# Differential attention on one core: every eighth maximum tile goes through ScalarE and GpSimd

## The reference, cut to what matters

```
q, k = rope(x @ Wq) * 8 ** -0.5, rope(x @ Wk)          # (b, 32, s, 8) each
scores = einsum('bhqd,bhkd->bhqk', q, k)                # 16 x 32 tables of 1024 x 1024
probs = softmax(scores, axis=-1)                        # fp32, over the keys
w = probs[:, :, 0] - lam * probs[:, :, 1]               # the two heads of a pair
attn = einsum('bhqk,bhkd->bhqd', w, v)                  # v has 16 columns
attn = attn * rsqrt(mean(attn ** 2) + eps) * subln_g * (1 - LAMBDA_INIT)
```

## Time and profile before

| | us |
|---|---|
| median of 3 runs (6433.96 to 6452.12) | 6438.76 |
| the profiled execution | 6450.77 |
| its span | 6449.0 |

### The profile page before, as it was taken

How to read it: one execution, slowest core, us unless ns; L and a number is a source line. 1 busy time by engine, 2 the same in 40 slices (tenths; PEclk the granted TensorE clock), 3 DMA queues, 4 the chain that set the end, 5 groups by cost and what they waited for, 6 DMA issues and landing times. The chain is left out here.

```text
span 6449.0 us, 136849 instructions
## 1 busy us (share of the span) xinstructions
PE 5794.4 (90%) x36560; PEld 1816.8 (28%) x36560; DVE 5879.4 (91%) x6456; ACT 4718.1 (73%) x8950; POOL 1947.2 (30%) x3270
## 2 busy tenths in 40 slices
PE   7776999999999999999999999999999999997775
PEld 4442222222222222222222222222222222224423
DVE  7998999999999999999999999999999999986716
ACT  4553878888788888887888888888878888783304
POOL 6774222222222222222222222222222222225506
PEclk8886999999999999999999999999999999998878
DMA  4554222222222222222222222222222222205688
GB/s 145 152 160 121 40 46 48 48 48 50 46 48 48 48 48 48 48 48 48 48 48 48 48 48 48 48 48 48 48 48 48 48 48 48 47 19 179 197 314 282
DMA packets 435720, 491.57 MB, mean 76 GB/s; under 512 B 106451, under 2 KB 288883, under 8 KB 435171
## 3 DMA queue, kind: packets, MB, share of 16 engines
q1 hardware_dynamic: 434147, 483.60, 31.2%
q10 hardware_dynamic: 1024, 0.53, 0.0%
HBM read 360.60 MB, written 123.21 MB: 75 GB/s over the span
## 5 line engine op out<-in xcount | busy, mean ns | idle before, releaser
L650 ACT ACTIVATE at_e<-at_ps_e 128x512 f32<-128x512 f32 x8192 | 4236.1, 602 | 944.1 <-PE at_ps_e L748 943.9
L664 DVE TENSOR_REDUCE at_largest<-at_ps_m 128x1 f32<-128x1024 f32 x4096 | 4777.2, 1211 | 156.4 <-PE at_ps_m L775 95.9
L775 PE MATMUL at_ps_m<-k_stack,q_stack 48*128 48x512 bf16 x8192 | 2725.2, 387 | 159.7 <-DVE at_largest L664 112.3
L748 PE MATMUL at_ps_e<-q_stack,k_stack 51*128 51x512 bf16 x8192 | 2478.6, 383 | 154.3 <-ACT at_e L650 69.1
L763 PE MATMUL at_ps_o<-at_e,at_v 128*32 128x512 f32 x16384 | 2255.2, 623 | 0.1
L748 PEld LDWEIGHTS at_ps_e<-q_stack,k_stack 51*128 51x128 bf16 x8192 | 624.5, 94 | 2520.6 <-ACT at_e L650 2216.6
L580 POOL TENSOR_TENSOR at_negated<-at_zeros,at_largest_t 128x32 f32<-128x32 f32 x256 | 64.8, 253 | 3244.3 <-DVE at_largest_t L671 3244.3
L775 PEld LDWEIGHTS at_ps_m<-k_stack,q_stack 48*128 48x128 bf16 x8192 | 620.1, 93 | 924.0 <-DVE at_largest L664 884.9
L763 PEld LDWEIGHTS at_ps_o<-at_e,at_v 128*32 128x32 f32 x16384 | 450.3, 149 | 525.5 <-issue 340.3
L615 POOL TENSOR_TENSOR at_rms<-at_mean_eps,at_minus_half 128x16 f32<-128x16 f32 x128 | 372.7, 2912 | 10.0
L429 PE MATMUL pr_ps_q<-pr_xn_t,pr_w 128*128 128x512 f32 x512 | 232.8, 597 | 1.5 <-issue 0.8
(11 more groups left out here) (128 smaller groups left out, 3082.2 us busy)
## 6 DMA issues: line engine op xcount, KB each, us to landing
k_stack<-k_parts SPq DMA_DIRECT2D x1536, 64.0 KB
q_stack<-q_parts SPq DMA_DIRECT2D x256, 192.0 KB
q_stack<-q_parts SPq DMA_DIRECT2D x256, 128.0 KB
w_first<-in_w SPq DMA_DIRECT2D x32, 1024.0 KB, 11.7
ex_w_second<-in_w SPq DMA_DIRECT2D x32, 1024.0 KB, 12.7
q_parts<-pr_parts SPq DMA_DIRECT2D x96, 256.0 KB, 2.9
k_parts<-pr_parts SPq DMA_DIRECT2D x96, 256.0 KB, 2.9
pr_x_in<-in_x SPq DMA_DIRECT2D x16, 1024.0 KB, 6.2
```

Source lines behind the costliest of these rows:

```text
L650: nc.scalar.activation(e[:, j % E_BUFS], ps_e[:, (HALVES * u + j) % SLOTS], ACT.Exp, scale=SCALE).then_inc(exp_done, 1)
L664: nc.vector.reduce_max(largest[:, u % 2, j // SIDE, j % SIDE:j % SIDE + 1], ps_m[:, j % 2], AX.X).then_inc(max_done, 1)
L748: nc.tensor.matmul(ps_e[:, (HALVES * u + j) % SLOTS], k_stack[rows, u, pair, c, kt * P:(kt + 1) * P], q_stack[rows, u, pair, c, half * HAL ...
L775: last = nc.tensor.matmul(ps_m[:, j % 2, half * HALF:(half + 1) * HALF], q_stack[rows, u, pair, c, t * P:(t + 1) * P], k_stack[rows, u, pa ...
```

## The change

Tries 0, 8, 16 and 24 of each quad are no longer reduced from PSUM by DVE. ACT copies each (128x1024) from `ps_m` to one of two buffers `fold_in`, after the second exponential of the period in which it is made. POOL folds it: high half minus low half, clamped at zero, added to the low half, which is the larger of the two; once on 512 and once on 256 columns; the result of 256 columns goes to `fold_out`. DVE takes the maxima of two such results in one reduction per side, in `turn_maxima`, and then waits for its own result before the transpose. Side 0 is turned at g = 10 (`TURN`) instead of 8. Maxima are now stored negated (the reductions negate), so `split` has four operations where it had five. POOL's order in a turn is: fold 0, `finish` of the previous quad, fold 1, split of side 0, folds 2 and 3, split of side 1. Try j waits for the copy instead of the reduction where try j-2 is a folded one; the counts in `max_done` are adapted. ACT's loop runs over 31 trips and writes out the last four quads, since the last quad has no tries to copy for.

```
--- before.py
+++ after.py
@@ -44,6 +44,7 @@
 LAMBDA_INIT = 0.8 - 0.6 * math.exp(-0.3 * 12)
 SCALE = HD ** -0.5
 EPS = 1e-5
+LARGEST = float(np.finfo(np.float32).max)
 THETA = 0.0001
 SWAP = [i ^ 1 for i in range(32)]
 
@@ -469,6 +470,18 @@
         BLK = 32
         BLOCKS = HALF // BLK
         loops = quads // BUFS - 1
+        FOLD_EVERY = 8
+        FOLDS = TRIES // FOLD_EVERY
+        WIDTH = S // 4
+        REDUCED = TRIES - FOLDS
+        TURN = TILES + 2
+
+        def folded(j):
+            return j % FOLD_EVERY == 0
+
+        def reduced_before(j):
+            return sum(not folded(i) for i in range(j))
+
         with ExitStack() as ctx:
             def sb(name, shape, dt=F32):
                 return ctx.enter_context(nc.sbuf_tensor("at_" + name, shape, dt))
@@ -480,7 +493,8 @@
             v = sb("v", [P, BUFS, 2, 2 * VD * TILES])
             e = sb("e", [P, E_BUFS, HALF])
             largest, largest_t = sb("largest", [P, 2, 2, BLK]), sb("largest_t", [P, BLK])
-            zeros, negated, rest = sb("zeros", [P, BLK]), sb("negated", [P, BLK]), sb("rest", [P, BLK])
+            zeros, rest = sb("zeros", [P, BLK]), sb("rest", [P, BLK])
+            fold_in, fold_out = sb("fold_in", [P, 2, S]), sb("fold_out", [P, 2, 2, WIDTH])
             parts = sb("parts", [P, PARTS, BLK], BF16)
             sums_t = sb("sums_t", [P, 2, BLOCKS, BLK])
             inverse = sb("inverse", [P, 2, BLOCKS])
@@ -507,8 +521,10 @@
             max_stored, inverse_done, attn_done, out_done = (sem("max_stored"), sem("inverse_done"), sem("attn_done"),
                                                              sem("out_done"))
             out_stored, pool_step = [sem("out_stored0"), sem("out_stored1")], sem("pool_step")
+            copied, fold_done, folds_read = sem("copied"), sem("fold_done"), sem("folds_read")
+            passed = sem("passed")
             ONES = 5
-            SPLIT_STEPS, FINISH_STEPS = 4, 10
+            SPLIT_STEPS, FINISH_STEPS, FOLD_STEPS = 3, 10, 5
             block = ctx.enter_context(nc.Block())
 
             @block.sync
@@ -577,16 +593,35 @@
                 def split(h, base):
 
                     pool.wait_ge(max_turned, h + 1)
-                    nc.gpsimd.tensor_tensor(negated[:], zeros[:], largest_t[:], ALU.subtract).then_inc(pool_step, 1)
                     if not (isinstance(h, int) and h == 0):
                         pool.wait_ge(max_stored, 16 * (P // BLK) * h)
-                    nc.gpsimd.tensor_tensor(parts[:, 0], zeros[:], largest_t[:], ALU.subtract).then_inc(pool_step, 1)
+                    nc.gpsimd.tensor_tensor(parts[:, 0], largest_t[:], zeros[:], ALU.add).then_inc(pool_step, 1)
+                    pool.wait_ge(pool_step, base + 1)
+                    nc.gpsimd.tensor_tensor(rest[:], largest_t[:], parts[:, 0], ALU.subtract).then_inc(pool_step, 1)
                     pool.wait_ge(pool_step, base + 2)
-                    nc.gpsimd.tensor_tensor(rest[:], negated[:], parts[:, 0], ALU.subtract).then_inc(pool_step, 1)
+                    nc.gpsimd.tensor_tensor(parts[:, 1], rest[:], zeros[:], ALU.add).then_inc(pool_step, 1)
                     pool.wait_ge(pool_step, base + 3)
-                    nc.gpsimd.tensor_tensor(parts[:, 1], rest[:], zeros[:], ALU.add).then_inc(pool_step, 1)
-                    pool.wait_ge(pool_step, base + 4)
                     nc.gpsimd.tensor_tensor(parts[:, 2], rest[:], parts[:, 1], ALU.subtract).then_inc(split_done, 1)
+
+                def fold(m, k, base):
+
+                    c, x = k // 2, fold_in[:, k % 2]
+                    pool.wait_ge(copied, FOLDS * m + k + 1)
+                    for width in (S // 2, S // 4):
+                        low, high = x[:, 0:width], x[:, width:2 * width]
+                        nc.gpsimd.tensor_tensor(high, high, low, ALU.subtract).then_inc(pool_step, 1)
+                        pool.wait_ge(pool_step, base + 1)
+                        pool.sem_inc(passed, 1)
+                        nc.gpsimd.tensor_scalar(high, high, LARGEST, 0.0, ALU.min, ALU.max).then_inc(pool_step, 1)
+                        pool.wait_ge(pool_step, base + 2)
+                        if width > WIDTH:
+                            nc.gpsimd.tensor_tensor(low, low, high, ALU.add).then_inc(pool_step, 1)
+                            pool.wait_ge(pool_step, base + 3)
+                            base = base + 3
+                        else:
+                            if not (isinstance(m, int) and m == 0):
+                                pool.wait_ge(folds_read, 2 * m + c - 1)
+                            nc.gpsimd.tensor_tensor(fold_out[:, c, k % 2], low, high, ALU.add).then_inc(fold_done, 1)
 
                 def finish(n, base):
 
@@ -619,36 +654,70 @@
 
                 def turn(n, rows, base):
                     if rows:
-                        for c in range(2):
-                            split(2 * (n + AHEAD) + c, base)
-                            base = base + SPLIT_STEPS
-                    finish(n, base)
-
-                for h in range(2 * AHEAD):
-                    split(h, SPLIT_STEPS * h)
+                        fold(n + AHEAD, 0, base)
+                        base = base + FOLD_STEPS
+                    finish(n - 1, base)
+                    base = base + FINISH_STEPS
+                    if rows:
+                        fold(n + AHEAD, 1, base)
+                        split(2 * (n + AHEAD), base + FOLD_STEPS)
+                        base = base + FOLD_STEPS + SPLIT_STEPS
+                        for k in (2, 3):
+                            fold(n + AHEAD, k, base)
+                            base = base + FOLD_STEPS
+                        split(2 * (n + AHEAD) + 1, base)
+
+                first = FOLDS * FOLD_STEPS + 2 * SPLIT_STEPS
+
+                def first_maxima(m, base):
+                    for c in range(2):
+                        for k in (2 * c, 2 * c + 1):
+                            fold(m, k, base)
+                            base = base + FOLD_STEPS
+                        split(2 * m + c, base)
+                        base = base + SPLIT_STEPS
+
+                first_maxima(0, 0)
+                first_maxima(1, first)
                 pool.wait_ge(lam_done, 1)
-                start, steps = 2 * AHEAD * SPLIT_STEPS, 2 * SPLIT_STEPS + FINISH_STEPS
+                start, steps = 2 * first, first + FINISH_STEPS
                 with hinted(nc, pool, 0, loops) as i:
                     for u in range(BUFS):
-                        turn(BUFS * i + u, True, start + steps * (BUFS * i + u))
+                        turn(BUFS * i + u + 1, True, start + steps * (BUFS * i + u))
                 for u in range(BUFS):
                     n = BUFS * loops + u
-                    turn(n, u < BUFS - AHEAD, start + steps * n - 2 * SPLIT_STEPS * max(0, u - (BUFS - AHEAD)))
+                    turn(n + 1, n + 1 + AHEAD < quads, start + steps * n - first * max(0, n + 1 + AHEAD - quads))
 
             @block.scalar
             def _(act):
+                act.sem_inc(exp_done, SLOTS)
+
+                def copy_trial(m, k):
+
+                    act.wait_ge(tries_done, TRIES * m + FOLD_EVERY * k + 1)
+                    if not (isinstance(m, int) and m == 0 and k < 2):
+                        act.wait_ge(fold_done, FOLDS * m + k - 1)
+                    nc.scalar.copy(fold_in[:, k % 2], ps_m[:, FOLD_EVERY * k % 2]).then_inc(copied, 1)
+
+                def turn(n, u, tries):
+                    for j in range(HALVES):
+                        act.wait_ge(scores_done, HALVES * n + j + 1)
+                        if j % QUAD == 0:
+                            act.wait_ge(sums_done, GROUPS * n + j // QUAD + 1 - E_GROUPS + E_GROUPS)
+                        nc.scalar.activation(e[:, j % E_BUFS], ps_e[:, (HALVES * u + j) % SLOTS], ACT.Exp,
+                                             scale=SCALE).then_inc(exp_done, 1)
+                        if tries and j % QUAD == 1 and folded(2 * (j // QUAD)):
+                            copy_trial(n + AHEAD, 2 * (j // QUAD) // FOLD_EVERY)
+
+                for k in range(FOLDS):
+                    copy_trial(0, k)
                 act.wait_ge(lam_dots, 1)
                 nc.scalar.activation(lam_exp[:], lam_dot[:], ACT.Exp).then_inc(lam_exps, 1)
-                act.sem_inc(exp_done, SLOTS)
-                with hinted(nc, act, 0, loops + 1) as i:
+                with hinted(nc, act, 0, loops) as i:
                     for u in range(BUFS):
-                        n = BUFS * i + u
-                        for j in range(HALVES):
-                            act.wait_ge(scores_done, HALVES * n + j + 1)
-                            if j % QUAD == 0:
-                                act.wait_ge(sums_done, GROUPS * n + j // QUAD + 1 - E_GROUPS + E_GROUPS)
-                            nc.scalar.activation(e[:, j % E_BUFS], ps_e[:, (HALVES * u + j) % SLOTS], ACT.Exp,
```

(24 more changed lines are left out.)

## The result

| | us |
|---|---|
| changed kernel, median of 4 runs (6599.47 to 6617.4) | 6606.98 |
| kernel before, median of 4 runs (6433.96 to 6452.12) | 6439.93 |
| ratio after / before | 1.0258 (1.0236 to 1.028) |
| the profiled execution of the changed kernel, its span | 6611.6, 6609.8 |

Slower by 167 us, 1.3 us for each of the 127 quads with tries. Forecast were 6579 and 1.13 a quad, inside a range of 6440 to 6720. All times and ratios here are of fast executions; one execution of the kernel of experiment 4 took 9511 us and is left out.

What follows compares the result with a forecast made beforehand. A ring through PE and ACT, not DVE, was taken as the bound. -0.90 + 1.78 + 0.25 = +1.13 us a quad, x 127 = +143, -3 at the start: +140 on 6438.8 gives 6579 us; range 6440 to 6720.

Steps and rivals of the forecast that it cites:

- the ring: Attention loop: PE and ACT instructions releasing each other, not through DVE, set 2.42 us a period, 38.77 us a quad.
- Rival 1, the busy shares: Attention loop: DVE at 97% limits and ACT's idle time takes the copies; faster, 6353 us; chance 0.11.
- rival 2: ACT's copies: the copy costs half, about no change, 6445 us; chance 0.05.
- The copy on the ring, 0.45: ACT, four copies a quad: each adds 0.45 us to the ring, 1.78 us a quad.
- DVE's 0.9 us: DVE's extra work (turnings, sums, reciprocal) lengthens some intervals: 0.9 us a quad, all that DVE costs before the change.
- the room at the gate: PE's even try waiting for DVE's reduction: 0.41 us of room, T+0.66 to T+1.07; T starts the period's third score.
- the 0.25: DVE's delays remaining after the change: 0.25 us a quad in place of 0.9.
- DVE's pace: DVE's reductions of tries from PSUM: 1.184 us each, from fourteen in 16.57 us.
- The turning: DVE turning a side's maxima: folded reduction 0.62, wait on its own result 0.1, then transpose; 0.87 us instead of 0.15.
- rival 3: POOL's folds late, DVE waiting: decides at a fold of 6.0 us; 6706 us at 6.5; chance 0.14.
- the end of 5.5: POOL's fold: forecast at 5.1 us, with ends 4.6 and 5.5.
- PE's stops without a releaser: PE's stops, 25 at weight loads, and what follows them: remaining 0.7 us of the 40.4 us quad, left unchanged.

Runs made afterwards that it cites:

- experiment 4: The changed kernel, but ACT copies only 16 of the 1024 columns of each folded try (maxima wrong): 6542 us, 1.0142 of the kernel before.
- experiment 2: Kernel before, tries 0, 8, 16, 24 reduced over 16 columns only and each exponential on 384 of 512 columns: 6328 us, 0.9811.
- experiment 3: Kernel before, with ACT also copying a constant 128x1024 SBUF tile at the change's four places, read by nobody; DVE reduces all 32 tries: 6615 us, 1.0258.
- experiment 1: Kernel before, with tries 0, 8, 16, 24 of each quad reduced over 16 of 1024 columns; no copy, no fold: 6427 us, 0.9967.
- experiment 5: The changed kernel, with side 0 turned in period 12 and POOL folding try 16 before that side's split: 6566 us, 1.0189 of the kernel before.
- experiment 7: The changed kernel, ACT copying only columns 512 to 1023, DVE reducing the rest from PSUM, side 0 turned in period 12: 6432 us, 0.9967 of the kernel before.
- experiment 6: The changed kernel, with one more 128x512 two-input POOL operation in each fold: 6890 us, 1.0686 of the kernel before.
- 8, half copy after extra work: The changed kernel with half copies of tries 0, 4, 16, 20, POOL folding to 64 columns, side 0 turned in period 10: 6362 us, 0.986 of before.

## Why the prediction was right, and where it was not

**The bound.** Right, and shown: the time follows ACT's instruction (experiments 2 and 3), not DVE's work (1). DVE stands close behind: half of what the shorter ring of experiment 2 would give came back as its delays. Rival 1, the busy shares, and rival 2 are out.

**The copy on the ring, 0.45.** Right: 0.46, four times a quad, in the change, and 0.48 with foreign data from SBUF. Of the parts, the pace is 0.89 (3024.35 to 3025.24) and not 0.93, and the group behind the copy makes up for it (2.12 for 2.06). An estimate by the formula of the Trainium skill (ScalarE: Activation LUTs, section What ACT_TABLE_LOAD costs) gives a pace of 0.946. That is above the 0.89 from PSUM and fits the 0.94 of experiment 3 from SBUF; on the ring it would make 0.47 a copy, which these runs can't tell from 0.45.

**DVE's 0.9 us and what is left of it.** The net was right by two errors that met, and that is luck. The step that failed is the room at the gate: I compared the opening of the gate (T+0.66) with the score behind it (T+1.07) and overlooked that the second half of the try must also run before the weighted sums. 0.19 is what there is. With 0.41 I had the relief worth 0.9 us a quad; alone it is worth 0.36 (experiment 1). In the change nearly all of the 0.9 goes all the same, because the copies lengthen the periods in which DVE would be late: alone they leave 0.12 (experiment 3), and with the copies made short the delays are back (experiment 4). So the 0.25 that I put against 0.9 was close to the 0.36 measured, for a reason that the text had only in half: I had seen the shift of T by 0.45 after each copy, and had not seen that this shift does nearly all of it. What the relief adds to it is worth about 0.1 us a quad (0.12 of delays in experiment 3, nothing left in experiment 5), less than the 0.32 that its dearer turning costs.

**DVE's pace.** 1.184 was wrong, 1.12 is right. I divided a stretch of fourteen reductions by fourteen although the first of each pair waits for its data; gaps of a few hundredths don't stand as idle time in a merged row. The sum should have warned me: 40.3 us of DVE's work do not fit into a quad of 39.67.

**The turning.** 0.87 forecast, 1.01 measured: the reduction 0.67 for 0.62, the wait on its own result 0.20 for 0.10. The 0.20 is not the price of that wait alone. In experiment 7 the wait for the side's reductions (`max_done`) stands ahead of the folded reduction instead of behind it, and the transpose starts 0.03 after the reduction's end (3004.77):

```profile
3004.09 0.68 DVE L740 TENSOR_REDUCE at_largest<-at_fold_out 128x2 f32<-128x514 f32 x1
3004.80 0.21 DVE L745 STREAM_TRANSPOSE at_largest_t<-at_largest 128x32 f32<-128x32 f32 x1
```

So the place of that one wait may have cost the change 0.17 us a turning; the two programs differ in more, and no run changes it alone. The dearer turning is the 0.32 at period 10 where 0.2 stood, and experiment 5 takes it away whole. With the 0.06 from four copies and the rest of the delays it makes up the difference of 0.17 us a quad, most of the 28 us between 6579 and 6607.

**POOL.** Covered, as forecast: by 0.34 us and not by 1 until DVE waits, and by 0.8 until it costs time (experiment 6). The 6.0 us at which rival 3 was to decide holds: of the 1.35 us added to a fold, half of 1.91, 0.96, reached the ring, so the loss began at 5.6 + 1.35 - 0.96 = 5.99. The fold's 5.6 is beyond the end of 5.5 that I had given. The two-input operations cost 1.27 and 0.73, not 1.058 and 0.614; the clamp was cheaper than taken (0.61 and 0.40) but starts 0.20 behind the operation before it. The row for 1.058 has one input that is broadcast, and the one for 0.614 reads the same tile twice. The addition of two different halves of a tile, 256 each, was in the profile of before and fitted (724 ns); I took the wrong neighbours:

```profile
L602 POOL TENSOR_TENSOR at_attn<-at_normed 128x256 f32<-128x256 f32 x128 | 92.7, 724 | 10.0
```

The rule of the Trainium skill (GPSIMD Engine Reference, section Engine selection) holds in its part on one input, roughly (0.61 for 512, where DVE's reduction of 512 from SBUF takes 0.67), and by it rival 3 does not occur. It didn't, but a fold is mostly two-input work, and at 5.6 us it was 0.4 short of where the rival begins.

**Small slips in the sums.** With a pace of 0.946 for 0.93 a quad is 0.064 longer, 8 us in all and not 13. Rival 2's own terms give 6449, the fold of 7.0 gives 6833, and the forecast's lower end about 6545 (for 6445, 6820 and 6535). None of them changes the forecast or a chance.

**What stays open.** PE's stops without a releaser differ between the programs by 14 us in 4000 at weight loads alone (experiment 1) and blur every comparison of small effects; where they come from wasn't tried. The table has, from one profiled execution of each kernel, the quad without a stop and the mean quad over 1000 to 5000 us (from the count of ACT's instructions). The difference is what the stretches with stops add; 0.1 us in it is 13 us of the whole time.

| kernel | quad without a stop | mean quad | difference |
|---|---|---|---|
| before | 39.66 | 40.41 | 0.75 |
| the change | 40.96 | 41.73 | 0.77 |
| 1, relief alone | 39.30 | 40.30 | 1.00 |
| 2, relief and short exponential | 38.52 | 39.48 | 0.96 |
| 3, copies alone | 40.81 | 41.76 | 0.95 |
| 4, small copy | 40.13 | 41.25 | 1.12 |
| 5, turned in period 12 | 40.60 | 41.31 | 0.71 |
| 6, longer fold | 42.87 | 43.98 | 1.11 |
| 7, half copy | 39.60 | 40.30 | 0.70 |
| 8, half copy after extra work | 39.20 | 39.84 | 0.64 |

The forecast had this difference unchanged at 0.7. For the change that came true (0.77), and with it the total; for five of the eight experiments it would not have.

## What to carry to other kernels

Find the ring before you count busy shares: take two starts of one instruction a period apart and follow what released what from one to the other. An engine outside the ring may be 97% busy and its relief worth 0.3%; an engine on the ring may be idle a fifth of the time and still have room only for what fits into the gap of one period (0.36 us of idle here, 0.48 from start to start: a copy of 512 columns fits, one of 1024 does not). Put relief next to the extra work that causes the delay, in the smallest size that fits, and not evenly; when you price a gate, follow everything that is queued behind it, not just the next instruction. And compare quads without stops before you explain a small difference in the total.

## What the runs showed of the hardware

A GpSimd operation on two different full inputs costs more than on one input read twice or broadcast: 128x512 fp32 1.27 against 1.06 us, 128x256 0.73 against 0.61. A clamp (two operations, one input) takes 0.61 and 0.40. It starts 0.20 after the operation whose result it waits for, against 0.08 or 0.09 ahead of a two-input operation; but in this program one more semaphore instruction (`passed`) stands ahead of each clamp, and no run tells the two apart. DVE's transpose starts 0.20 after the end of the small reduction that it waits for in the change, and 0.03 after it in experiments 7 and 8, which have one wait fewer between the two. An ACT copy of 128x1024 starts 0.89 before the next exponential when it reads PSUM and 0.94 when it reads SBUF, and costs 0.46 and 0.48 on the ring.
